# A decoder layer in post-norm form: linear attention's steps reordered, values from rounded and remainder parts, middle norm and last projection elsewhere

## The reference, cut to what matters

```
def linear_attention(x):
    Q, K, V = x @ W_q.T, x @ W_k.T, x @ W_v.T
    S = (Q K^T inside chunks of 32 tokens) * mask(decay ** distance)
    out = sigmoid(x @ W_g.T) * (S @ V) @ W_o.T + x
def cross_attention(q_in, ctx):              # 16 heads of 64
    qw, kw, vw = q_in @ Wq + bq, ctx @ Wk + bk, ctx @ Wv + bv
    a = softmax(qw kw^T / 8 over the 512 keys, masked)
    return (a @ vw) @ Wo + bo
def ffn(x):                                  # 1024 hidden, ternary weights
    h = bitlinear(x, w_fc) + gate * (x @ v.T @ fast_b.T @ u.T)
    return bitlinear(relu(h) ** 2, w_proj)
x = layernorm(x + linear_attention(x))
x = layernorm(x + cross_attention(x, ctx))
x = layernorm(x + ffn(x))
```

## Time and profile before

| | |
|---|---|
| median of 3 runs | 1316.46 us (1314.57 to 1319.10) |
| the profiled execution | 1318.03 us, its span 1315.9 us |
| PE busy | 1272.9 us, 97% |
| DVE, ACT, POOL busy | 923.5, 794.7, 775.7 us (70%, 60%, 59%) |
| chain that ended last | PE 89% of the span |
| transfers | 43.08 MB, 33 GB/s on average |

### The profile page before, as it was taken

One profiled execution on the slowest core, in us unless ns is written; L12 is line 12 of the kernel. 1 busy time (PEld: TensorE's weight loads), 2 busy tenths in 40 slices (PEclk: granted clock), 3 DMA queues, 4 the chain that ended last, 5 costly groups with the idle time before them and its releaser, 6 DMA issues.

```text
span 1315.9 us, 21104 instructions
## 1 busy us (share of the span) xinstructions
PE 1272.9 (97%) x6836; PEld 850.6 (65%) x6836; DVE 923.5 (70%) x1809; ACT 794.7 (60%) x1063; POOL 775.7 (59%) x449
## 2 busy tenths in 40 slices
PE   6999999999999999999999999999999998899997
PEld 5767765657566656665666666657566655577775
DVE  6678876684766677576757656684775677678887
ACT  2354445574656566565657565575666666679885
POOL 3504218995877687677958767794876787300000
PEclk9999998999999999999999999999999999899998
DMA  6311211100100110011011001100200110010101
GB/s 214 113 35 62 82 47 20 19 2 17 42 11 1 32 34 0 16 32 18 0 28 37 2 0 48 18 0 16 48 2 0 33 33 2 20 61 33 64 17 48
DMA packets 99392, 43.08 MB, mean 33 GB/s; under 512 B 77169, under 2 KB 82049, under 8 KB 99345
## 3 DMA queue, kind: packets, MB, share of 16 engines
q1 hardware_dynamic: 98528, 39.33, 12.1%
q0 software_dynamic: 816, 3.15, 0.7%
HBM read 29.59 MB, written 12.58 MB: 32 GB/s over the span
## 4 chain that ended last, share of the span: by engine, by line
PE 89%; POOL 3%; DVE 3%; ACT 2%; issue 1%; SPq 1%; DMA 1%; POOLq 0%; ACTq 0%; DVEq 0%
PE ps L1310 16%; PE ps L1285 14%; PE ps L48 11%; PE ps L50 10%; PE ps L49 10%; PE ps L1301 4%; PE ps L1289 4%; PE ps L1343 2%; PE ps L1344 2%; PE ps L1342 2%; PE ps L1319 2%; PE ps L1732 2%; PE ps L1733 2%; POOL acc L931 2%; PE ps L716 1%
## 5 line engine op out<-in xcount | busy, mean ns | idle before, releaser
L1139 DVE CUSTOM_DVE_ANT_0 junk<-ps,mask 128x512 bf16<-128x512 f32 x504 | 314.9, 686 | 89.3 <-PE ps L1301 88.0
L1005 ACT ACTIVATE prob<-ps,mcol 128x1024 f32<-128x1024 f32 x256 | 282.0, 1116 | 140.1 <-PE ps L1289 135.2
L931 POOL TENSOR_TENSOR acc<-acc,prob 128x1024 f32<-128x1024 f32 x128 | 307.0, 2399 | 11.6 <-ACT prob L1005 0.3
L928 POOL TENSOR_TENSOR acc<-prob 128x1024 f32<-128x1024 f32 x64 | 155.3, 2426 | 220.8 <-ACT prob L1005 219.5
L1310 PE MATMUL ps<-prob,v_b 128*64 128x512 f32 x1024 | 246.2, 602 | 0.0
L945 POOL TENSOR_TENSOR acc_lo<-acc,acc_hi 128x1024 f16<-128x1024 f32 x64 | 138.7, 2168 | 5.1
L1310 PEld LDWEIGHTS ps<-prob,v_b 128*64 128x64 f32 x1024 | 68.1, 137 | 108.8 <-issue 75.9
L1285 PE MATMUL ps<-q_hi,k_hi 64*128 64x512 f32 x512 | 115.1, 445 | 4.2 <-DVE rs L225 4.0
L1301 PE MATMUL ps<-k_hi,q_hi 64*128 64x512 f32 x504 | 101.0, 396 | 3.8 <-DVE nmx L1139 3.8
L1285 PE MATMUL ps<-q_hi,k_lo 64*128 64x512 f32 x512 | 102.3, 395 | 0.0
L1285 PE MATMUL ps<-q_lo,k_hi 64*128 64x512 f32 x512 | 102.1, 394 | 0.0
(11 more groups left out here) (230 smaller groups left out, 2881.9 us busy)
## 6 DMA issues: line engine op xcount, KB each, us to landing
shift<-nmx SPq DMA_DIRECT2D x512, 0.5 KB, 2.0
x_in<-in_xT SPq DMA_DIRECT2D x8, 512.0 KB, 3.7
x_scratch<-x_a SPq DMA_DIRECT2D x8, 512.0 KB, 2.8
raw<-in_cT SPq DMA_DIRECT2D x8, 512.0 KB, 3.7
raw<-x_scratch SPq DMA_DIRECT2D x8, 512.0 KB, 3.9
y<-x_scratch SPq DMA_DIRECT2D x8, 512.0 KB, 3.7
y_scratch<-y SPq DMA_DIRECT2D x8, 512.0 KB, 2.8
y_c<-y_scratch SPq DMA_DIRECT2D x8, 512.0 KB, 3.8
```

The lines of the kernel that those rows point to most:

```text
L928: pool.tensor_tensor(total, prob[:, 0], prob[:, 1], ALU.add).then_inc(acc_out, 1)
L931: pool.tensor_tensor(total, total, prob[:, kt], ALU.add).then_inc(acc_out, 1)
L1005: act.activation(prob[:, i].rearrange("p h t -> p (h t)"), SCORE[i % 2].rearrange("p h t -> p (h t)"), ACT.Exp, scale=SCALE, bias=mcol[:, ...
L1139: dve.tensor_tensor_reduce(junk[:, t % 2, h], SMAX[t % 2][:, h], mask[:], -1.0, -LOWEST, ALU.add, ALU.min, nmx[:, p % 2, t, h:h + 1]).then ...
```

## The change

Linear attention: the values become a `split_matmul` of the same x parts that gates and queries use, with WvT split into hi and lo; W_o is split later. `variance` and `deviation` of a sequence move into the step after the next one (`variance(b-2)`, `deviation(b-2)` in step b), and with them `root` and `scale_x1`, so that in VectorE's order `root(b-2)` stands ahead of `finish_y(b-1)` and `split_x(b+1)` ahead of `subtract_mean(b-1)`. The attend products wait for each half of the values by itself. The first gates are computed in the order in which the parts of x come. The sum over the second ternary weight moves from before step 1 to behind `gated(1)`, and the product with it, `scale_means`, from the end of step 1 into step 2, ahead of `queries(2)`. SyncE stores x1 one step later.

Cross attention: GpSimd in place of VectorE centres Wo, and VectorE's sum over it stands among the first maxima. In the last step the weights of the hidden layer are split behind pair 0 in place of pair 6, sequence 0's middle norm is computed in the fifth pair in place of the seventh, with tiles of its own, and its last remainder in the last pair; the ternary weights are cast after the last pair's sums.

Feed-forward: `last_sums` goes from behind `hidden(0, 0)` to behind `hidden(0, 4)`, and `last_project` from behind `hidden(0, 5)` into the second product, into the banks of the hidden layer.

```diff
             act.activation(gate[:], G, ACT.Sigmoid).then_inc(g_out, 1)
+            if not (isinstance(b, int) and b < 2):
+                act.preload_act_table_set("natural_log_exp_and_others")
+
+        def query_copies(b):
...
         front(0)
...
+        front(1)
+        query_copies(1)
         act.wait_ge(f_sum, 1)
         act.activation(wabs[:].rearrange("p k (j n) -> p (k j) n", n=D), wpr[:], ACT.Abs).then_inc(f_abs, 1)
-        front(1)
+        values(1)
         square(0)
-        values(1)
...
         with act.Fori(2, B - 1, 2) as i:
             for b in (i, i + 1):
                 front(b)
+                deviation(b - 2)
+                query_copies(b)
+                values(b)
                 square(b - 1)
-                values(b)
-                deviation(b - 1)
...
+        split_weight(2, "WvT", raw["WvT"][:])
...
         def step(b, par, last):
+            if b > 1:
+                root(b - 2)
             finish_y(b - 1, 1 - par)
             mask_scores(b)
+            if b > 1:
+                scale_x1(b - 2)
+            if not last:
+                split_x(b + 1, 1 - par)
             subtract_mean(b - 1)
             sum_squares(b - 1)
-            if not last:
-                split_x(b + 1, 1 - par)
             gated(b)
             if b == 1:
+                sum_out_weights()
                 scales()
             if b in (2, 3):
                 low_rank(b - 2)
-            if not last:
-                root(b - 1)
...
+        def sum_out_weights():
+            dve.wait_ge(f_abs, 2)
+            dve.tensor_reduce(psc[:], wabs[:].rearrange("p k (j n) -> p n (k j)", n=D), AX.X,
+                              ALU.add).then_inc(f_sum, 1)
...
+        split_x(1, 1)
         mask_scores(0)
-        split_x(1, 1)
-
+        split_weight(3, "WoT", raw["WoT"][:])
+        gated(0)
...
-                mm = full_matmul(pe, vb[:, t], [(x[:, par, k, t * P:(t + 1) * P], wv[:, k, :]) for k in range(DK)])
+                tok = slice(t * P, (t + 1) * P)
+                mm = split_matmul(pe, vb[:, t], [(x_hi[:, par, k, tok], x_lo[:, par, k, tok], w_hi["WvT"][:, k, :],
+                                                  w_lo["WvT"][:, k, :]) for k in range(DK)])
...
             pe.wait_ge(s_out, b + 1)
-            pe.wait_ge(v_out, 2 * b + 2)
-            for m in range(DK):
-                for t in range(NT):
-                    mm = pe.matmul(QO[:, m, t * P:(t + 1) * P], v[:, t, m * P:(m + 1) * P], s[:, t],
-                                   start=True, stop=True)
+            for n in range(2):
+                pe.wait_ge(v_out, 2 * b + n + 1)
+                for m in range(DK):
+                    for t in (2 * n, 2 * n + 1):
+                        mm = pe.matmul(QO[:, m, t * P:(t + 1) * P], v[:, t, m * P:(m + 1) * P], s[:, t],
+                                       start=True, stop=True)
                 mm.then_inc(o_ps, 1)
...
             gates(b, par)
+            if b > 1:
+                variance(b - 2)
+            if b == 2:
+                scale_means()
             queries(b, par)
...
             outputs(b - 1)
             scores(b, par)
-            values(b, par, (0,))
+            values(b, par, (0, 1))
+            if b == B - 1:
+                values(b, par, (2, 3))
+            if b == 1:
+                pe.wait_ge(f_mid, 1)
             mean(b - 1)
-            values(b, par, range(1, NT))
+            if b < B - 1:
+                values(b, par, (2, 3))
             attend(b)
-            variance(b - 1)
...
-            if b == 1:
-                scale_means()
...
+        def centre_output_weight(half):
+            rows = slice(half * HALF, half * HALF + HALF)
+            means = wo_mean[:, rows].rearrange("p (k o) -> p k o", o=1).to_broadcast([P, HALF, D])
+            pool.wait_ge(wo_summed, 2)
+            pool.tensor_tensor(wo[:, rows], wo[:, rows], means, ALU.subtract).then_inc(wo_centred, 1)
...
-                if first and p in (1, HALF):
-                    split_output_weight(p // HALF)
+                if first and p == HALF:
+                    split_output_weight(1)
                 if p == PAIRS - 3 and not last:
...
-                if last and p == PAIRS - 2:
+                if last and p == PAIRS - 1:
                     pool.wait_ge(q_ps, PAIRS * B)
                     f.ternary(pool)
 
...
-                if last and p == HALF - 2:
-                    f.norm2_square(act, 0, 0)
-                if last and p == PAIRS - 2:
-                    f.weights_hi(act)
...
+                if last and p == 0:
+                    f.weights_hi(act)
+                    f.norm2_square(act, 0, 0)
+                if last and p == HALF:
+                    f.norm2_root(act, 0, True)
...
-                    f.weights_lo(dve, 1)
...
+                if last and p == HALF:
+                    f.root2(dve, 0)
+                    projected_out(b, 0, (0,))
+                    f.scale2(dve, 0, 0)
+                    projected_out(b, 0, (1,))
+                    f.split2_hi(dve, 0, 0)
+                elif p == HALF:
+                    projected_out(b, 0)
...
+        first_maxima(1)
+        dve.tensor_reduce(wo_sum[:], wo[:], AX.X, ALU.add).then_inc(wo_summed, 1)
+        dve.wait_ge(wo_summed, 1)
+        dve.tensor_scalar(wo_mean[:], wo_sum[:], 1.0 / D, None, ALU.mult).then_inc(wo_summed, 1)
+        first_maxima(2)
+        first_maxima(3)
         la.root(B - 1)
         la.scale_x1(B - 1)
-        dve.tensor_reduce(wo_sum[:], wo[:], AX.X, ALU.add).then_inc(wo_centred, 1)
-        dve.wait_ge(wo_centred, 1)
-        dve.scalar_tensor_tensor(out=wo[:], in0=wo_sum[:].rearrange("p (k o) -> p k o", o=1).to_broadcast([P, PAIRS, D]),
-                                 scalar=-1.0 / D, in1=wo[:], op0=ALU.mult, op1=ALU.add).then_inc(wo_centred, 1)
...
-                if last and p == PAIRS - 1:
+                if last and p == HALF + 1:
                     pe.wait_ge(f.rs2_out, 1)
...
+            hidden(b, 5, first)
             if first:
                 ca.last_attended_hi()
-            for i in (3, 4, 5):
...
-                ca.last_sums()
-            for i in (1, 2, 3):
+            for i in (0, 1, 2, 3):
...
             if first:
+                ca.last_sums()
...
-            if first:
-                ca.last_project()
...
             if first:
-                pe.wait_ge(ca.o_out, 2 * DK * B)
+                pe.wait_ge(f.tern_out, 1)
...
-            if last:
+            if first:
+                for m in range(DK):
+                    project(b, m, range(0, 4))
+                pe.wait_ge(f.relu_out, 6)
+                ca.last_project()
+                for m in range(DK):
+                    project(b, m, range(4, 6))
```

More of the change, by code:

```diff
@@ L288, in linear_attention_phase @@
     s = sb(ctx, "s_masked", [P, NT, P], F32)
-    raw = {w: sb(ctx, w + "_l0", [P, DK, D], F32) for w in ("WvT", "Wq", "Wk", "WgT", "WoT")}
-    wv = raw["WvT"]
+    raw = {w: sb(ctx, w + "_l0", [P, DK, D], F32) for w in ("WvT", "WgT", "WoT")}
+    with ExitStack() as product:
+        raw.update({w: sb(product, w + "_l0", [P, DK, D], F32) for w in ("Wq", "Wk")})
+    w_hi["WvT"] = sb(ctx, "WvT_l0_hi", [P, DK, D], F32R)
+    w_lo["WvT"] = sb(ctx, "WvT_l0_lo", [P, DK, D], F32R)
     for w in ("M", "WgT"):
@@ L712, in attend, with first_gates @@
             pe.wait_ge(s_out, b + 1)
-            pe.wait_ge(v_out, 2 * b + 2)
-            for m in range(DK):
-                for t in range(NT):
-                    mm = pe.matmul(QO[:, m, t * P:(t + 1) * P], v[:, t, m * P:(m + 1) * P], s[:, t],
-                                   start=True, stop=True)
-                mm.then_inc(o_ps, 1)
+            for n in range(2):
[4 more added lines that the diff above has]
+                                       start=True, stop=True)
+                mm.then_inc(o_ps, 1)
+        def first_gates():
+            for l, r, ready in ((w_hi, x_hi, 1), (w_lo, x_hi, 1), (w_hi, x_lo, 2)):
+                pe.wait_ge(x_split, ready)
+                for m in range(DK):
+                    for k in range(DK):
+                        mm = pe.matmul(G[:, m], l["WgT"][:, k, m * P:(m + 1) * P], r[:, 0, k],
+                                       start=(l is w_hi and r is x_hi and k == 0), stop=(r is x_lo and k == DK - 1))
+            mm.then_inc(g_ps, 1)
         pe.wait_ge(w_split, 2)
-        gates(0, 0)
+        first_gates()
         pe.wait_ge(w_split, 4)
         queries(0, 0)
+        pe.wait_ge(w_split, 6)
+        values(0, 0, (0, 1))
         scores(0, 0)
-        pe.wait_ge(w_in, 32)
-        values(0, 0, range(NT))
+        values(0, 0, (2, 3))
         attend(0)
@@ L898, in batch @@
                     load_residual(b)
-                if p == 3 and last:
+                if p == PAIRS - 2 and last:
+                    sp.wait_ge(k_ps, PAIRS * B)
                     load_norm(1)
@@ L1077, in batch @@
```

(15 more changed lines are left out.)

190 lines of the change are left out of this document (99 added, 91 removed).

## The result

The changed kernel takes 1305.68 us in the median of 5 runs (1303.62 to 1308.15), the one before 1316.61 (1314.57 to 1320.26) in the same measurement: a ratio of 0.9908, 95% interval 0.9888 to 0.9928, a gain of about 11 us. The prediction was 1293.5 with a range of 1281 to 1304. The sign was right, the size was not, and the time lies outside the range.

What follows compares the result with a forecast made beforehand. TensorE, busy 97% of the span, bounds the kernel; gains come from its waits, low clock and removed products. 4.7 + 5.9 + 12.9 - 0.5 = 23.0 us off 1318.0 gives 1295.0, 1293.5 for the median; range 1281 to 1304.

Steps and rivals of the forecast that it cites:

- linear attention up to the passage: Lead of 7.7 us at the passage, less 3.0 for VectorE operations meeting GpSimd's: 4.7 us gained.
- first pair: Cross attention's start: wait of 2.94 us and the low clock behind it (3.0) go, 5.9 us gained.
- head: From the last pair's first product to feed-forward step 1: 34.7 us in place of 47.65, 12.9 us gained.
- Last batch: Splitting the hidden layer's weights in pair 0, where pairs are full, costs 0.5 us.
- Opening: Start of linear attention: scores(1) at 31.2 in place of 40.30, 9.1 us earlier.
- Step 2: Linear attention: queries(2) waits 5.9 us for the sum behind gated(1), leaving 3.2 us of lead at scores(2).
- Later steps: Linear attention: a chain through gate_used, table load, root and finish_y binds at 18.8 us a step against TensorE's 16.5.
- The rival of heavier contention: Linear attention: all eight VectorE-GpSimd meetings and those of the table loads fall on the chain; 1300 us, chance 0.17.
- the rival of the half gain at the head: Feed-forward's start gives half, as GpSimd's adds end late or sequence 0's root delays ScalarE's exponentials; 1300 us, chance 0.11.
- The drain behind a table load: Linear attention: each of a step's two table loads costs a further stop, chain 16 us longer; 1309 us, chance 0.03.
- a TensorE at half speed in the steps: Linear attention: new idle pieces put TensorE at 1.2 GHz, 49 us if half the products; 1343 us, chance 0.06.
- the first rival: Linear attention: the chain does not bind and steps run at TensorE's 16.5 us; 1281.5 us, chance 0.13.

Runs made afterwards that it cites:

- the experiment: Changed kernel with the sum over the second ternary weight ahead of gated(1) in place of behind it: 1299.29 us, ratio to before 0.9849.
- two experiments: Changed kernel with sequence 1's variance product behind hidden(0, 6): 1300.03 us; changed kernel with GpSimd's ternary cast held back until VectorE has its sum: 1300.94 us.
- the kernel with three edits: Changed kernel with early sigmoid table load, second-weight sum ahead of gated(1), sequence 1's variance product behind hidden(0, 6): 1294.8 us, ratio to before 0.9813.
- the one with all five: Changed kernel with early table load, sum ahead of gated(1), variance product behind hidden(0, 6), ternary cast and Wo's split held back: 1292.42 us, ratio 0.9801.

## Why the prediction was too low

By the traces the terms of the sum came out as 1.1 us for 4.7 (linear attention up to the passage), 4.5 for 5.9 (first pair), 0.5 for -0.5 (last batch) and 8.0 for 12.9 (head), with 0.3 more behind it: 14.4 for 23.0. The step that failed is the price of the meetings of VectorE with GpSimd. The prediction allows 3.0 us for them in linear attention and nothing in the terms of 5.9 and of 12.9, and the last is the largest miss.

*Opening: right.* 8.8 us of lead for 9.1.

*Step 2: the wait right, the clock behind it missing.* The wait was 5.63 for 5.9. Behind it the granted clock was 0.52, and the products up to `queries(2)` took 4.92 us where the full clock gives 2.62. These 2.3 us were not in the sum; other small terms gave some of them back, and the lead left was 2.2 for 3.2. The sum's place behind `gated(1)` costs 4.0 us, which the experiment gives back.

*Later steps: right, the meetings slightly mis-sized.* The chain through `gate_used`, the table load and the root exists (steps of 18.3 without GpSimd's work, 17.2 when the load also leaves it, for 18.8 and 17.5). The sentence "I count two as falling on the chain with no slack, 2.8" counted too few meetings: five stand in steps 4 and 5 alone. But not all of their length reaches TensorE: without GpSimd's work the steps are 3.5 us shorter, and 3.0 had been taken. VectorE and GpSimd in the changed kernel:

```profile
95.40 1.88 DVE L577 SCALAR_TENSOR_TENSOR rs_a<-rs_a,est_a 128x512 f32<-128x512 f32 x1
97.21 1.27 DVE L542 SCALAR_TENSOR_TENSOR y_a<-x_in,ps 128x512 f32<-128x512 f32 x2
98.51 1.54 DVE L547 TENSOR_TENSOR tile_sum_a<-y_a 128x512 f32<-128x512 f32 x1
99.98 0.68 DVE L566 TENSOR_TENSOR s_masked<-ps,dmask 128x512 f32<-128x512 f32 x1
100.58 2.80 DVE L584 SCALAR_TENSOR_TENSOR x_a<-dev_a,rs_a 128x1024 f32<-128x1024 f32 x1
...
94.57 2.17 POOL L413 TENSOR_TENSOR wfc_raw<-above,wfc_raw 128x1024 f32<-128x1024 bf16 x1 [29.42 <-DVE wfc_raw L618]
96.82 2.70 POOL L415 TENSOR_TENSOR wfc_raw<-wfc_raw,scale 128x1024 f32<-128x1024 f32 x1
99.59 2.71 POOL L417 TENSOR_TENSOR wfc<-wfc,wfc_raw 128x1024 f32<-128x1024 f32 x1
```

Each of GpSimd's three operations holds up one of VectorE's: the root ends 0.5 us behind the first, the sum 0.5 behind the second, `x_a` 1.1 behind the third (102.30 and 103.38). That is 1.2 + 0.85 + 1.6 = 3.6 us of VectorE's time in step 4 and 2.4 in step 5. They are not spread by chance over the stage: `compare_in` starts GpSimd at a fixed place, and the change has moved `root`, `finish_y` and `scale_x1`, the very instructions with two inputs in SBUF, behind it. I knew the new order and GpSimd's durations, and should have laid GpSimd's row beside VectorE's. The hand-made layout also had 17.6 us for the step from scores(4), which took 20.36, and 18.3 without GpSimd's work. From scores(2) to scores(7) 95.6 us passed for 92.0, or 95.0 with the allowance.

*Passage and first pair: a gain turned into a wait.* In step 7 the gated result sets the next products on both sides: from scores(7) to the first product with `og_hi` pass 13.86 us before (170.78 in its trace) and 13.78 after. What TensorE saves there became the wait of 2.59 us, a lower clock followed it (0.76 up to the product with bo; later products of the same kind last 0.63 us against 0.39), and the lead fell from 2.7 to 1.1 at the product with bo. This was not in the sum, which had 0.5 more lead here. VectorE's work ahead of that wait meets GpSimd too:

```profile
156.03 2.68 DVE L547 TENSOR_TENSOR tile_sum_a<-y_a 128x512 f32<-128x512 f32 x1
...
165.26 1.52 DVE L597 CAST og_hi<-sq_a 128x1024 fp32r<-128x1024 f32 x1
```

Each takes 0.69 where nothing stands beside it. No experiment moved these two, so what they cost TensorE is not shown. The first pair gave 4.5 of its 5.9 us (the lead is 5.5 behind its weighted values, 201.49 against 207.03): the centring left VectorE as forecast, and the split of Wo on GpSimd came to lie beside the root and x_a (1.6 us, shown by holding it back), which the term had at nothing.

*Head of the feed-forward: 8.0 for 12.9.* The wait of 4.00 and those for the last sums went, as forecast. The term left out VectorE beside `acc_lo` and the cast: 3.3 to 3.7 of the 4.9 us that are missing, by two experiments (waiting and low clock together). The cause of the rest stays open.

*Last batch:* 0.5 lost was forecast, 0.5 was gained between the first pair and the last; which of the edits there did it was not tried.

The meetings that the experiments removed thus cost 3.5 us in the steps, 1.6 at the first pair and about 3.5 at the head, 8.6 in all, where 3.0 had been taken. The rival of heavier contention (1300, 0.17) had the cause, but looked for it in the steps of linear attention, where only 0.5 us more than allowed came; the rival of the half gain at the head (1300, 0.11) had the place, with other causes (GpSimd's adds, the root). I had set them as separate cases and let the range end where each alone ends; one cause lay under both, and the time came out beyond it, at 1305.7. The drain behind a table load did not come (in the changed kernel a load starts at 88.93 and the sigmoid at 90.22), nor did a TensorE at half speed in the steps: the granted clock is 1.00 from 60 to 154 us. Two slips of arithmetic change nothing: the first rival's five steps of 2.3 us end at 1282.0 and not 1281.5, and the chances sum to 1.00 before the 0.02 for something unseen.

On the meetings, the Trainium skill ("SBUF — State Buffer", section "SBUF: two separate sides") says that the pair of ports is locked for a whole instruction when VectorE has two inputs in SBUF and GpSimd reads SBUF. The rows agree in both directions: `y_a` and `s_masked`, with an input in PSUM, kept 0.64 and 0.68 us beside the same operations of GpSimd that held the others up.

## What to carry to other kernels

When an instruction of VectorE with both inputs in SBUF moves, lay GpSimd's timeline beside its new place: the loser waits for the end of the other's instruction, which cost 0.9 to 1.6 us each time in the rows of steps 4 and 5, and where GpSimd is started by a VectorE instruction just ahead, it happens in every such step. Do so for every term of the sum, not for one stage alone. When two rivals have the same cause, sum them for the range's end instead of weighing them apart. And a chain that has just become the bound takes back what is saved elsewhere: a single edit on it (the early table load) showed half of its worth until the meeting behind it was gone too.

## What was not expected of the hardware

An instruction of 0.69 us on VectorE took 1.54, 1.88, 1.95 or 2.02 us beside GpSimd's operations of 2.2 to 2.7, and one of 1.22 took 2.80, the same within 0.01 in both steps 4 and 5 and in the kernel with the early load. The low clock behind a wait does not follow from the wait's length alone. Behind 5.63 us it cost 2.3 us. Behind about 2.1 us at the same place it cost nothing in the kernel with three edits (2.62 us for the stretch) and 1.7 in the one with all five (4.31 at 0.60). Behind 2.59 us at the passage it cost 1.6, behind 2.65 nothing. Each is one execution. A difference of this size between two kernels may thus be chance, and their waits have to be compared with the clock beside them.
